# The last gather-and-sum sweep of a two-layer graph network: eight products per signal, a longer ring, no credits for gathers

## The reference, cut to what matters

```
h = jnp.maximum(_layernorm(x, axis=-1), 0.0)
msgs = h[src]
summed = jax.ops.segment_sum(msgs, dst, num_segments=n)
deg = jax.ops.segment_sum(jnp.ones((msgs.shape[0],)), dst, num_segments=n)
mean_aggr = summed / jnp.maximum(deg, 1.0)[:, None]
x = x + mean_aggr @ w_l.T + h @ w_r.T + b
```

## Time and profile before

| | us |
|---|---|
| median of 3 runs | 6955.18 |
| profiled execution | 7020.43 |
| its span, first to last instruction | 7019.1 |
| last sweep: first gather starts | 4613.9 |
| last sweep: first add of DVE, last add of DVE | 4684.4, 6966.2 |
| busy in the whole span: PE, DVE, POOL | 4234.5, 3509.5, 3811.9 |

### The profile page before, as it was taken

How to read it: one execution, slowest core, us unless ns; L and a number is a source line. 1 busy time by engine, 2 the same in 40 slices (tenths; PEclk the granted TensorE clock), 3 DMA queues, 4 the chain that set the end, 5 groups by cost and what they waited for, 6 DMA issues and landing times. The chain is left out here.

```text
span 7019.1 us, 78246 instructions
## 1 busy us (share of the span) xinstructions
PE 4234.5 (60%) x16860; PEld 3154.7 (45%) x16861; DVE 3509.5 (50%) x9168; ACT 1150.0 (16%) x4356; POOL 3811.9 (54%) x3800
## 2 busy tenths in 40 slices
PE   3677676767676777738999996643333333333336
PEld 2555555555555555524444443533333333333336
DVE  6444444444444444478999999842222222222224
ACT  1111111111111111105666662210000000000000
POOL 2555555555555555515655551436666666666661
PEclk8888888888888888868999998655555555555555
DMA  6333333333333333313343331111111111111111
GB/s 92 92 97 95 94 100 94 101 91 96 91 101 92 100 95 96 95 34 108 112 111 109 112 111 38 40 31 23 23 23 23 23 23 23 23 23 23 22 23 25
DMA packets 633421, 478.51 MB, mean 68 GB/s; under 512 B 452184, under 2 KB 460504, under 8 KB 632972
## 3 DMA queue, kind: packets, MB, share of 16 engines
q1 hardware_dynamic: 468378, 258.75, 14.6%
q0 software_dynamic: 104800, 108.55, 8.2%
q10 hardware_dynamic: 60050, 109.22, 4.2%
HBM read 350.07 MB, written 126.05 MB: 68 GB/s over the span
## 5 line engine op out<-in xcount | busy, mean ns | idle before, releaser
L509 POOL DMA_INDIRECT ZR<-hD,mS x1664 | 1579.3, 949 | 1368.8 <-SPq L494 912.4
L1146 POOL DMA_INDIRECT BIG<-h2D,mS x1564 | 1476.5, 944 | 893.7 <-issue 452.3
L1170 PE MATMUL PS<-BIG,ZR 128*128 x3328 | 791.4, 424 | 1494.4 <-DVE ZR L465 1141.7
L539 PE MATMUL PS<-Wz,R 128*128 128x264 f32 x3328 | 1197.0, 445 | 819.5 <-issue 404.2
L1170 PEld LDWEIGHTS PS<-BIG,ZR 128*128 128x128 f32 x3328 | 736.4, 328 | 1549.4 <-issue 1548.3
L567 DVE SCALAR_TENSOR_TENSOR PS<-PS,a 128x528 f32<-128x528 f32 x832 | 595.0, 715 | 1568.8 <-remote 855.7
L1189 DVE TENSOR_TENSOR BIG<-BIG,PS 128x64 f32 x1664 | 362.4, 218 | 1709.2 <-remote 1316.9
L540 PE MATMUL PS<-BIG,R 128*128 x3328 | 1138.3, 427 | 0.0
L539 PEld LDWEIGHTS PS<-Wz,R 128*128 128x128 f32 x3328 | 648.5, 217 | 965.2 <-issue 889.6
L804 PE MATMUL PS<-R,ZR 128*128 128x329 f32 x3328 | 1027.5, 469 | 28.1 <-DVE ZR L739 23.2
L790 POOL TENSOR_TENSOR R<-ZR,R 128x768 f32<-128x768 f32 x416 | 616.1, 1481 | 423.0 <-ACT R L776 421.1
(11 more groups left out here) (226 smaller groups left out, 2522.4 us busy)
## 6 DMA issues: line engine op xcount, KB each, us to landing
zD<-ZR ACTq DMA_DIRECT2D x416, 256.0 KB
ZR<-zD SPq DMA_DIRECT2D x416, 256.0 KB, 2.6
R<-relD SPq DMA_DIRECT2D x105, 512.0 KB
ZR<-ea SPq DMA_DIRECT2D x1664, 32.0 KB
ZR<-hD,mS POOLq DMA_INDIRECT x1664
BIG<-h2D,mS POOLq DMA_INDIRECT x1564
AL<-hD SPq DMA_DIRECT2D x28, 224.0 KB, 2.8
lmS<-lmD SPq DMA_DIRECT2D x106, 32.0 KB, 1.8
```

What stands on the lines that cost most here:

```text
L509: Q.indirect_dma_start(zring[:, j % 32, 0, :], None, hD, bass.IndirectOffsetOnAxis(mS[:, j // 16, j % 16:j % 16 + 1], 0)).then_inc(hs[q], 16)
L539: P.matmul(m, zo[:, p % 2, (j % 2) * 128:(j % 2) * 128 + 128], Wz, start=True, stop=False)
L1146: Q.indirect_dma_start(BIG[:, j * F:j * F + F], None, h2D, bass.IndirectOffsetOnAxis(mS[:, (j // 16) % 4, j % 16:j % 16 + 1], 0)).then_inc ...
L1170: ins = P.matmul(bank3(j // 4)[:, j % 4, :], oh[:, (j // 4) % 4, j % 4, :], rows, start=True, stop=True)
```

## The change

In the last sweep a PSUM bank now takes the products of eight slots instead of four, so PE signals once for eight slots, and waits before each eight for a free bank (`b3_free`, four at the start, given by DVE after its eight adds). DVE makes the one-hots of six groups of eight (48 slots) before the loop, and in the loop those of six groups ahead, into a ring of its own of eight groups (`oh3`) in `BIG`. The ring of gathered tiles has 256 places (R3) instead of 128. The credits `gf` are gone; what still holds POOL back is `i3_rdy`, the table of 16 slots' indices, of which four are there at the start. The wait for `i3_rdy` now stands ahead of the instruction that readies the semaphores. Since `oh3` lies over `H2`, DVE too now waits for the store of `h2D` (`dH2`) before it goes on behind the normalization.

```diff
+R3 = 256
-    v(V.tensor_scalar(tI3, tI[:, 0, :], 127, None, ALU.bitwise_and))
+    v(V.tensor_scalar(tI3, tI[:, 0, :], R3 - 1, None, ALU.bitwise_and))
...
-    gf, o3_rdy, a3_rdy, c3_acc, go3, i3f, i3_rdy, r3f, r3_rdy = flows("p3_", 9)
-    S.sem_inc(gf.s, 7)
+    o3_rdy, a3_rdy, b3_free, c3_acc, go3, i3f, i3_rdy, r3f, r3_rdy = flows("p3_", 9)
+    S.sem_inc(b3_free.s, 4)
...
-    dH2.wait(Q)
+    dH2.wait(Q, V)
...
                 if j % 16 == 0:
                     m = min(4, n // 4 - q)
+                    i3_rdy.take(Q)
                     Q.inc_swdge_sem(g1[q % 16:q % 16 + m], [64] * m, mode="sub")
                     Q.sem_inc(go3.s, 1)
-                    i3_rdy.take(Q)
-                if j % 4 == 0:
-                    gf.take(Q)
...
-        with Q.Fori(0, NG3 // G):
-            some(G)
-        some(NG3 % G)
+        with Q.Fori(0, NG3 // R3):
+            some(R3)
+        some(NG3 % R3)
...
+    oh3 = BIG[:, R3 * F:R3 * F + 8192].rearrange("p (o s n) -> p o s n", o=8, n=128)
+    AHEAD = 6
+    def bank3(o):
+        return PS[:, o % 4, :].rearrange("p (s f) -> p s f", f=F)
+    def onehots3(o, k):
+        at = 8 * (o % 2) + 4 * k
+        return V.tensor_tensor(oh3[:, o % 8, 4 * k:4 * k + 4, :], bc(iota_ps.unsqueeze(1), [128, 4, 128]),
+                               bc(mR[:, (o // 2) % 4, at:at + 4].unsqueeze(2), [128, 4, 128]), ALU.is_equal)
...
                 if j % 4 == 0:
                     P.wait_ge(g1[j // 4], 64)
+                if j % 8 == 0:
                     o3_rdy.take(P)
-                ins = P.matmul(bank3(j // 4)[:, j % 4, :], oh[:, (j // 4) % 4, j % 4, :], rows, start=True, stop=True)
-                if j % 4 == 3:
+                    b3_free.take(P)
+                ins = P.matmul(bank3(j // 8)[:, j % 8, :], oh3[:, j // 8, j % 8, :], rows, start=True, stop=True)
+                if j % 8 == 7:
                     ins.then_inc(a3_rdy.s, 1)
...
+            for o in range(8):
+                if o % 2 == 0:
+                    r3_rdy.take(V)
+                for k in range(8):
+                    if k % 4 == 0:
+                        to = [ahead(V, AG[:, ds(vt(8 * o + k + n) * F, F)]) for n in range(4)]
+                    if k == 0:
+                        a3_rdy.take(V)
                     c3_acc.take(V)
+                    V.tensor_tensor(to[k % 4], to[k % 4], bank3(o)[:, k, :], ALU.add).then_inc(c3_acc.s, 1)
+                    if k == 3:
+                        onehots3(o + AHEAD, 0)
+                onehots3(o + AHEAD, 1).then_inc(o3_rdy.s, 1)
+                V.wait_ge(c3_acc.s, c3_acc.n + 1).then_inc(b3_free.s, 1)
+                if o % 2 == 1:
                     V.sem_inc(i3f.s, 1)
                     V.sem_inc(r3f.s, 1)
```

More of the change, by code:

```diff
@@ L1130, in tables3 @@
             close(i3f, r3f)
-        r3f.take(A)
-        A.copy(mR[:, 0, :], rel3[:, 0:16]).then_inc(r3_rdy.s, 1)
+        for half in range(3):
+            r3f.take(A)
+            A.copy(mR[:, half, :], rel3[:, 16 * half:16 * half + 16]).then_inc(r3_rdy.s, 1)
     def gathers3():
@@ L1148, in some @@
                                      ).then_inc(g1[q % 16], 16)
-            close(i3_rdy, gf)
-        with Q.Fori(0, NG3 // G):
-            some(G)
-        some(NG3 % G)
+            close(i3_rdy)
+        with Q.Fori(0, NG3 // R3):
+            some(R3)
+        some(NG3 % R3)
         Q.sem_inc(go3.s, NHALF - (NG3 + 15) // 16)
-    def bank3(q):
-        return PS[:, q % 4, 0:4 * F].rearrange("p (s f) -> p s f", f=F)
+    oh3 = BIG[:, R3 * F:R3 * F + 8192].rearrange("p (o s n) -> p o s n", o=8, n=128)
[6 more added lines that the diff above has]
+                               bc(mR[:, (o // 2) % 4, at:at + 4].unsqueeze(2), [128, 4, 128]), ALU.is_equal)
     def sums3():
         with P.Fori(0, NS // 64) as i:
-            pt = Table(P, tabD[2:3, :], i, "sl", (G - 1) * F, 64)
+            pt = Table(P, tabD[2:3, :], i, "sl", (R3 - 1) * F, 64)
             for j in range(64):
@@ L1168, in sums3 @@
                     P.wait_ge(g1[j // 4], 64)
+                if j % 8 == 0:
                     o3_rdy.take(P)
-                ins = P.matmul(bank3(j // 4)[:, j % 4, :], oh[:, (j // 4) % 4, j % 4, :], rows, start=True, stop=True)
-                if j % 4 == 3:
+                    b3_free.take(P)
+                ins = P.matmul(bank3(j // 8)[:, j % 8, :], oh3[:, j // 8, j % 8, :], rows, start=True, stop=True)
+                if j % 8 == 7:
                     ins.then_inc(a3_rdy.s, 1)
-            close(o3_rdy)
+            close(o3_rdy, b3_free)
     def adds3():
-        r3_rdy.take(V)
-        for q in range(2):
-            onehots(q).then_inc(o3_rdy.s, 1)
+        for o in range(AHEAD):
+            if o % 2 == 0:
+                r3_rdy.take(V)
+            onehots3(o, 0)
+            onehots3(o, 1).then_inc(o3_rdy.s, 1)
         close(r3_rdy)
@@ L1182, in adds3 @@
             vt = Table(V, bT3, i, "ub", NB - 1, 64)
[L1183 to L1187, removed]
-                    c3_acc.take(V)
[L1189 to L1194, removed]
+            for o in range(8):
+                if o % 2 == 0:
+                    r3_rdy.take(V)
+                for k in range(8):
[3 more added lines that the diff above has]
+                        a3_rdy.take(V)
+                    c3_acc.take(V)
+                    V.tensor_tensor(to[k % 4], to[k % 4], bank3(o)[:, k, :], ALU.add).then_inc(c3_acc.s, 1)
[4 more added lines that the diff above has]
+                if o % 2 == 1:
                     V.sem_inc(i3f.s, 1)
```

## The result

The changed kernel is slower: 7130.28 us (median of 4 runs, 7102.45 to 7222.24) beside 6959.1 us of the kernel before on the same chip (4 runs, 6949.84 to 7001.57), ratio 1.022 with a 95% interval of 1.0158 to 1.0283, so slower for certain, and by about 2%. The run of 7222.24 us, 1.7% above the fastest, is in the median but not in the ratio. The profiled execution took 7102.45 us (before: 7020.43). From the first gather to the last add the sweep takes 2463 us instead of 2352, 111 more. In this pair the stages ahead of it ended 29 us earlier, which is scatter: in the traces of this kind the first gather starts anywhere between 4569 (h1) and 4621 us (g4). The pair of profiles is thus only 82 us apart where the medians are 171 apart.

The account below looks back on a forecast made before the run. The sweep was taken as bound by PE's signals arriving late while POOL gathers, with only 8 slots of products before DVE. Gathers -145 us (start included), end +22, sum -123: 6955 to 6832 us; range 6700 to 7015.

Parts of the forecast that it names:

- Rival B: Last sweep: long gather runs starve PE's signals, 9.3 us pause after every 48 gathers; 7007 us, chance 0.28.
- The failed step: Last sweep: after a run's first 15 us one signal passes every 15 us, giving 1.327 us per slot.
- For it: half as many signals: Last sweep: fewer PE signals as an argument that they pass in time, every 10 us or better.
- rival A: Last sweep: signals pass in time, POOL never pauses after the start, 1.25 us per gather; 6704 us, chance 0.25.
- B's price: Last sweep under Rival B: 9.3 us pause per 48 slots, 1.444 us per slot; gathers +30, end +22.
- The start: Sweep's start: DVE's large add waits 13.2 us for the store, first add at 4742 not 4684.4; costs 16 us.
- DVE's group: Last sweep: DVE needs 5.2 to 5.4 us per eight slots, 0.66 per slot, hidden while signals are in hand.
- The end: After the last gather: DVE adds about 155 slots at 0.66 us, 101 us instead of 78, +22.
- At nothing: Terms put at zero: ring of 256, POOL's longer loop, order of `i3_rdy` and semaphore readying, PE's waits and clock.

Follow-up runs that it names:

- h1: The changed kernel with source indices 0 to 127 in a row for every slot, transfers still indirect; 7119.89 us (one run).
- g4: g1 with a signal of PE after every four products instead of eight, DVE waiting for both; 6998.2 us, ratio 0.9971 to the kernel before.
- f2: The kernel before without credits for gathers, e1's kernel repeated on a chip where before takes 6976.09 us; 7194.05 us, ratio 1.0307.
- g1: The changed kernel with five credits, one per eight slots, given when DVE sees a group, and DVE's store wait behind its own part; 7002.61 us, ratio 0.9976.
- e4: The changed kernel with SP loading consecutive rows by plain transfers instead of POOL's gathers (other data), where before takes about 5931 us; 4882.64 us.
- e1: The kernel before without credits for gathers, ring of 256, banks as before, in a series where before takes 5931.43 us; 5933.18 us, ratio 0.9995.
- f1: The changed kernel itself, repeated on another chip where before takes 6976.09 us; 7103.96 us, ratio 1.018.
- h3: g1 with three credits at the start instead of five; 6987.0 us, ratio 0.9966 to the kernel before.
- e3: The changed kernel with POOL resting for three memsets after every 32 gathers, where before takes about 5931 us; 6109.57 us, ratio 1.0294.
- g3: The changed kernel with POOL loading consecutive rows by plain transfers instead of indirect ones (other data); 5639.53 us (one run).
- f4: e4's kernel, SP's plain loads in place of POOL's gathers, repeated where before takes 6976.09 us; 5591.4 us (one run).
- f3: e3's kernel, POOL resting after every 32 gathers, repeated where before takes 6976.09 us; 7079.82 us, ratio 1.0129.

## Why the prediction was wrong

What bounds the kernel before was read rightly: adds late only while POOL gathers, and POOL's pause as what lets them go. Rival B, signals starving in a long run with a pause after every 48 gathers, is what happened: 32 pauses, "about 30" were named. The steps one by one:

- **The failed step** is "I take one passing every 15 us once the first 15 us of a run are over". The first 15 us were right (POOL resumes at 4841.80, the fourth group starts at 4855.09). Behind them the next group started 34.4 us later (4889.52) and the one after that only 7.8 us after POOL had stopped; the longest such gaps in the sweep are 44.1 us. The forecast counted signals; what is slow is each of PE's instructions, 1.4 us apart. A bank of four is 16 of them, by this some 22 us, and f2 has 21.0; a bank of eight is 32, by this 45 us, and the changed kernel has 44.1. The gap doubles with the bank, to about the 45 us that the prediction gave as the point from which B decides. In the kernel before POOL stopped before a gap could grow so long: the earlier trace rows have 8.8 and 15.9 us. That signals of the own part passed 12 us apart agrees with this in size: a pair there is five matmuls and their loads, which at 1.4 us each would be 14 us.
- **"For it: half as many signals"**, said for rival A, was worth nothing: g4 doubles them at no cost. g4, with 208 signals more than g1, took 4.4 us less (6998.2 and 7002.61), within the scatter of both. The rule of the Trainium skill, TensorE: Matmul & The Clock Gate, "The cost: per-tile semaphore tail", prices each increment at 26.3 ns, an estimate of 5.5 us for 208; g1 and g4 cannot show so little, and it is no part of this loss.
- **B's price** was too low: 9.3 us per pause, 1.444 us per slot, 7007 us. The pauses behind the first are 9.3 to 15.3 us, 12.5 on average, of which 0.3 stands between any two gathers: 60 us of gathers and some 12.2 of pause make a cycle of 48 slots 72.2 us, 1.504 per slot. In the cycle shown DVE gets its next group 7.8 us after POOL's stop, where B took 3.4. Some 3 us on each of 31 pauses are about 90 us. In the profiles the gathers take 111 us longer than before (2385 and 2274 us from the first to the end of the last), where B had 30; the end, which B had at 22, is nothing. The medians lie 171 us apart, and what is beyond 111 us is not in this pair of profiles: the profiled run of before lies 65 us above the median that the prediction started from, and no trace tells in which stage.
- **The start** was right. DVE's large add waits for the store and begins 1.0 us before the first gather (forecast 0.2), the first add comes 127 us after the first gather (4712.00; forecast 128):

```profile
4583.89 6.69 DVE L1099 TENSOR_TENSOR AL<-AL,PS 128x6272 f32<-128x6272 f32 x1 [12.37 <-DMA h2D<-BIG]
4584.93 1.06 POOL L1146 DMA_INDIRECT BIG<-h2D,mS  x1 [96.32 <-issue]
...
4704.03 7.26 DVE L1165 TENSOR_TENSOR BIG<-PS,mR 128x512 f32<-128x512 f32 x12
...
4712.00 0.98 DVE L1205 TENSOR_TENSOR BIG<-BIG,PS 128x64 f32 x4 [0.71 <-PE PS L1181]
```

- **DVE's group** was forecast at 5.2 to 5.4 us; two of its groups in hand follow each other in 3.4 us (4842.95, 4846.38), and 4.4 us on average where nothing else limits (e4). Hidden, as said.
- **The end** was forecast 22 us longer and is the same: last gather to last add 78.6 us, before 79.4. DVE had 140 slots left when the last gather ended, not about 155, and took 0.55 us for each, not 0.66; in the earlier trace rows it took 9.80 us for 16 slots, in e4 twice 4.4.
- **At nothing**: the clock is 0.50 in both. The ring, POOL's longer loop and the order of `i3_rdy` are in e1 too, which takes 0.9995 of before in the short kind.

How much of the loss is which part: taking the credits away costs 3.1% (f2, with the ring and the order of waits that go with it), and the wide banks with one-hots further ahead give back some 1.3 of these (f1 beside f2, 7103.96 and 7194.05 us in one series). With few credits on top (h3) the change is worth 0.34%, give or take 0.2. So the gain that was to come from POOL's pauses turned into a longer wait of the same kind: the pauses of 3.9 us were the time in which PE's work came through.

What stays open: what in an indirect transfer of POOL holds PE up; what the 62 instructions between PE's recorded start and its signal wait for, and whether the taking of the trace itself has a part in it, since no run is known to be without one; why a program meets it in some series and not in others; whether the share of time or the length of a run decides. The changed kernel itself was not timed in the short kind; e1 and e3 let one expect no loss there, and that is argued only. That the lateness in the kernel before is this same trickle is argued too, from f2 and h3: f2 differs from it by the missing credits and what goes with them, and has the gap of 21.0 us with PE's starts looking normal. PE is never more than two quads in front there, 16 matmuls, so its records have no room to show the trickle. The Trainium skill, Perfetto Trace Analysis, "Per-instruction lifecycle: what the profiler-reported window actually captures", has the end of a matmul as an estimate; h3's group, 14.5 us late behind such an end, agrees with that. That the starts of 34 more matmuls look normal meanwhile does not follow from it and stays open.

## What to carry to other kernels

An idle time is not a loss until it is known what the other engines do in it: before taking a pause away, look whether late work lands just behind it. When a delay is seen only as a late signal, ask whether it grows with the number of signals or with the instructions in front of each, since a wider batch halves the number of signals and doubles the instructions for each. Limit how far a gathering engine may run ahead by credits given for what is seen to be done, and try two sizes; between five and eight lay 2.2% here.

## What the hardware showed that was not expected

- In the long kind, beside a long row of indirect gathers on POOL, PE's instructions start 1.4 us apart, weight loads and matmuls alike, instead of some 0.22 us per pair; 0.7 us apart shortly after the gathers stop. Signals come 21.0 us apart for 16 such instructions (f2) and 44.1 us for 32 (the changed kernel), and lie 31 matmuls behind PE's recorded starts.
- Plain transfers issued by POOL at 0.526 us apart (g3), loads issued by SP (f4) and memsets on POOL (f3) do not do this, indirect ones of rows in a row do (h1).
- The same program took 5931 and 5947 us in two series and 6959 to 7015 us in the others, with the same duration (0.94 us) and pitch (1.25 us) of a gather.
